# Split expert weights from DRAM tables, and a feed-forward that stays channel-major until its end

## The reference

```python
mod = (silu(c) @ wmod).reshape(32, 6, 1, 256)
sa, ca, ga, sb, cb, gb = ...          # ga, gb: magnitude at least 0.25
h = layernorm(x) * (1 + ca) + sa
S = scan(a * s + (1 - a) * h_t)       # along time
x = x + ga * (S @ W.T + b + depthwise_conv5(h) + conv_b)
h = layernorm(x) * (1 + cb) + sb
sel = argmax(softmax(gelu(h[:, -1] @ Wp1 + bp1) @ Wp2 + bp2))
g = gelu(h @ W1[sel] + b1[sel])       # 256 -> 512 channels
out = (g @ W2[sel] + b2[sel]) @ Wo + bo
x = x + gb * (h + 0.3 * out)
```

## Time and profile before

| | us |
|---|---|
| median of three runs (775.01 to 775.7) | 775.07 |
| span of the profiled execution | 773.5 |
| first up matmul of row 0 starts | 82.47 |
| first up matmul of row 31 starts | 754.22 |
| one row in the steady part (ACT's xn of 399.75 to that of 421.61) | 21.86 |

### The profile page before, as it was taken

The page is one execution under the profiler, slowest core; times in us unless marked ns, Lnnn a source line. Parts: engine busy times, 40 slices in busy tenths (PEclk is TensorE's granted clock), DMA queues, the critical chain, the costliest instruction groups (busy, mean ns, idle before and its releaser), DMA issues.

```text
span 773.5 us, 14701 instructions
## 1 busy us (share of the span) xinstructions
PE 703.6 (91%) x4343; PEld 589.4 (76%) x4343; DVE 656.7 (85%) x1357; ACT 540.6 (70%) x919; POOL 605.6 (78%) x556
## 2 busy tenths in 40 slices
PE   5987899999999999999999999999999999999986
PEld 5776777788777777888777777887777777887775
DVE  1777799999999999999999999999999999999821
ACT  1246877778777777787777777787777777787653
POOL 2003888888888988888898888888899888888775
PEclk9999999999999999999999999999999999999999
DMA  9630022211111121111111222101122221211011
GB/s 309 219 106 17 31 63 62 63 59 37 44 48 62 61 61 61 61 48 41 41 53 61 61 61 61 61 33 44 45 61 61 61 61 61 60 34 44 21 36 55
DMA packets 47391, 48.93 MB, mean 63 GB/s; under 512 B 2874, under 2 KB 44793, under 8 KB 47361
## 3 DMA queue, kind: packets, MB, share of 16 engines
q1 hardware_dynamic: 46736, 46.96, 19.6%
q10 hardware_dynamic: 624, 1.61, 0.6%
HBM read 31.73 MB, written 16.83 MB: 63 GB/s over the span
## 4 chain that ended last, share of the span: by engine, by line
POOL 35%; ACT 31%; issue 19%; PE 7%; ACTq 3%; DVE 3%; POOLq 1%; DMA 1%; DVEq 0%
ACT xn L442 15%; POOL up_w L393 9%; POOL down_w L403 9%; POOL rstd L367 7%; POOL ve L365 4%; ACT up_w L480 4%; ACT hid L542 3%; ACT hid_hi L548 3%; ACT g_hi L516 3%; ACT g L511 2%; POOL nmr L371 2%; ACTq L475 2%; PE Q L827 2%; POOL mr L369 2%; PE TR L797 1%
## 5 line engine op out<-in xcount | busy, mean ns | idle before, releaser
L642 DVE SCALAR_TENSOR_TENSOR Y<-h,taps,Y 128x512 f32<-128x512 f32 x320 | 226.4, 743 | 36.9 <-PE Y L933 33.3
L411 POOL TENSOR_TENSOR g_lo<-g,g_hi 128x512 fp32r<-128x512 f32 x128 | 161.2, 1279 | 1.6 <-ACT g_hi L516 1.6
L833 PE MATMUL Q<-down_w,g_lo 128*128 128x256 f32 x512 | 158.4, 309 | 0.0
L835 PE MATMUL Q<-down_w,g_hi 128*128 128x256 f32 x512 | 144.5, 282 | 0.0
L834 PE MATMUL Q<-down_w,g_hi 128*128 128x256 f32 x512 | 144.5, 282 | 0.0
L442 ACT ACTIVATE xn<-x,nmr,rstd 128x256 f32<-128x256 f32 x128 | 66.4, 589 | 87.9 <-POOL nmr L371 87.9
L393 POOL TENSOR_TENSOR up_w<-up_all,up_w 128x1024 fp32r<-128x1024 f32 x32 | 76.5, 2390 | 46.8 <-ACT up_w L480 46.8
L833 PE MATMUL U<-hid_hi,up_w 128*128 128x512 f32 x256 | 103.6, 405 | 0.0
L835 PE MATMUL U<-hid_hi,up_w 128*128 128x512 f32 x256 | 101.3, 396 | 0.0
L834 PE MATMUL U<-hid_lo,up_w 128*128 128x512 f32 x256 | 101.1, 395 | 0.0
L511 ACT ACTIVATE g<-U,b_w 128x512 f32<-128x512 f32 x128 | 87.4, 683 | 17.2 <-PE U L835 14.0
(11 more groups left out here) (115 smaller groups left out, 1584.2 us busy)
## 6 DMA issues: line engine op xcount, KB each, us to landing
x_sb<-in_L_attn_x_dram SPq DMA_DIRECT2D x32, 512.0 KB, 4.8
out_dram<-o_sb SPq DMA_DIRECT2D x64, 256.0 KB, 2.2
g<-in_L_ffn_W_dram SPq DMA_DIRECT2D x8, 512.0 KB, 4.3
up_all<-in_L_ffn_W_dram SPq DMA_DIRECT2D x1, 4096.0 KB, 16.8
gb_bc<-gate_table SPq DMA_DIRECT2D x32, 128.0 KB, 4.0
x<-in_L_wmod_dram ACTq DMA_DIRECT2D x2, 384.0 KB, 3.5
beta_w<-beta_table SPq DMA_DIRECT2D x32, 2.0 KB
xn<-in_L_wmod_dram ACTq DMA_DIRECT2D x1, 384.0 KB, 5.0
```

Source lines behind the costliest of these rows:

```text
L411: nc.gpsimd.tensor_tensor(g_lo[:, f], g[:, f], g_hi[:, f].bitcast(f32), ALU.subtract).then_inc(g_lo_ready, 1)
L642: ins = nc.vector.scalar_tensor_tensor(out=Y[c][:, :], in0=h[:, c, k:k + T], scalar=taps[:, c, k:k + 1], in1=Y[c][:, :], op0=ALU.mult, op1 ...
L833: mm(out_, w_lo, m_hi, start=start, stop=False)
L835: return mm(out_, w_hi, m_hi, start=False, stop=stop)
```

## The change

All per-row weight work moves to a set-up. For each expert ACT and POOL split W1 once, and the hi and lo parts are written by SP to a DRAM table `up_table` (1 MB per expert; its last columns hold b1 and 0.3 * (b2 @ Wo + bo)); the combined down weights are split by ACT and DVE and written to `down_table` (1 MB per expert). Per row, SP waits for the router and fetches both halves: two DMAs of about 1 MB into buffers that alternate by row.

The down product becomes channel by time: 24 matmuls of 512 columns, the start being four matmuls that add `hid_lo` and `hid_hi` through an fp32r identity. Gate and bias are applied by one ACT operation per half on the way out of PSUM (into `rT`), then eight PE transposes (t4) go back to times, and DVE adds x in place. x stays in one ring of six row buffers; `gate_table`, `modc`, `gb_bc`, `o_sb` and `x1` are gone.

The `lo` part of the scan moves from DVE to POOL. The norm's two trivial steps (add EPS, negate the mean) move from POOL to DVE, which leaves POOL two operations per norm. The loop is written out in full, slots -3 to 31, with the rows set one slot further ahead. The modulation is made by six fp32 matmuls of 512 columns and twelve transposes. The order inside the slot is new for every engine.

```diff
-EXPERTS_AT = {(-2, "middle"): (0,), (-1, "start"): (1, 2), (-1, "fill"): (3, 4), (-1, "middle"): (5,),
-              (0, "start"): (6,), (0, "fill"): (7,)}
+EXPERTS_AT = {(-3, "t1"): (0, 1), (-2, "t1"): (2, 3), (-2, "t2"): (4,),
+              (-1, "router"): (5,), (-1, "t1"): (6,), (-1, "t2"): (7,)}
...
+    for e in range(E):
+        split_out(e)
+        if e + 2 < E:
+            load_w1(e + 2)
...
+        if e in (1, 2, 3):
+            load_w2(e + 1)
+        if e == 5:
+            load_w2(5)
+    for e in range(4):
+        down_out(e)
+    load_w2(6)
+    sp.wait_ge(s_comb, 2 * 5)
+    load_x(3)
+    load_w2(7)
+    for e in range(4, E):
+        down_out(e)
...
+        wait(sp, up_done, FC * (r - 1))
+        wait(sp, gelu_out, FC * (r - 1))
+        wait(sp, gbeta_ready, r - 1)
+        wait(sp, down_done, DC * (r - 1))
+        sp.wait_ge(sel_ready, r + 1)
+        e = sp.value_load(sel8[0:1, par, 0:1], min_val=0, max_val=E - 1)
+        sp.dma_start(up_w[:, par].bitcast(f32), up_table[bass.ds(e, 1)].rearrange("o p n -> p (o n)")).then_inc(up_loaded[par], 16)
+        sp.dma_start(down_w[:, par].rearrange("p k n -> p (k n)").bitcast(f32),
+                     down_table[bass.ds(e, 1)].rearrange("o p n -> p (o n)")).then_inc(down_loaded[par], 16)
...
+        pool.wait_ge(stats_ready, r + 1)
+        wait(pool, used, TT * r)
+        nc.gpsimd.tensor_tensor(rstd[:, :], ve[:, :], minus_half[:, :], ALU.pow).then_inc(step, 1)
+        pool.wait_ge(step, r + 1)
+        nc.gpsimd.tensor_tensor(nmr[:, :], nm[:, :], rstd[:, :], ALU.mult).then_inc(ready, 1)
...
+    def slot(i):
+        if row(i + 3):
+            norm(i + 3, stats1_ready, xn1_ready, nm1, ve1, rstd1, nmr1, rstd1_step, norm1_ready)
+        if i == -3:
+            for e in range(4):
+                w1_lo(e)
+        if i == -2:
+            for e in range(4, E):
+                w1_lo(e)
+        if row(i):
+            g_low(i, 0)
+            g_low(i, 1)
+        if row(i + 1):
+            r = i + 1
+            wait(pool, up_done, FC * (r - 1))
+            for c in range(DC):
+                pool.wait_ge(hid_hi_ready, DC * r + c + 1)
+                nc.gpsimd.tensor_tensor(hid_lo[:, r % 2, c], hid[:, c], hid_hi[:, r % 2, c].bitcast(f32),
+                                        ALU.subtract).then_inc(hid_lo_ready, 1)
...
+            wait(pool, oT_ready, DC * i)
...
+            g_low(i, 2)
+            g_low(i, 3)
+        if row(i + 2):
+            norm(i + 2, stats2_ready, xn2_ready, nm2, ve2, rstd2, nmr2, rstd2_step, norm2_ready)
+        if row(i + 3):
+            r = i + 3
+            wait(pool, mix_done, DC * r)
+            for c in range(DC):
+                pool.wait_ge(S_hi_ready, DC * r + c + 1)
+                nc.gpsimd.tensor_tensor(S_lo[:, c], S[:, c], S_hi[:, c].bitcast(f32), ALU.subtract).then_inc(S_lo_ready, 1)
...
+        wait(act, s_comb, 2 * (e - 1))
+        if e == 6:
+            act.wait_ge(s_w1_lo, 7)
...
+    def slot(i):
+        if row(i):
+            g_high(i, 0)
+        if row(i + 1):
+            r = i + 1
+            wait(act, hid_lo_ready, DC * r)
+            for c in range(DC):
+                act.wait_ge(t3_done, DC * r + c + 1)
+                nc.scalar.activation(hid[:, c], TR[c][:, :], ACT.Identity, bias=col(SB + c, r),
+                                     scale=col(CB + c, r)).then_inc(hid_ready, 1)
+        if row(i):
+            gelu(i, 1)
+            g_high(i, 1)
+        if row(i + 1):
+            r = i + 1
+            act.wait_ge(r_nav, r + 1)
+            nc.scalar.activation(nav[:, :], TR[0][:, 0:1], ACT.Gelu, bias=vecs[:, V_BP1:V_BP1 + 1]).then_inc(nav_ready, 1)
+            wait(act, up_done, FC * (r - 1))
+            for c in range(DC):
+                act.wait_ge(hid_ready, DC * r + c + 1)
+                nc.scalar.copy(hid_hi[:, r % 2, c], hid[:, c]).then_inc(hid_hi_ready, 1)
+        for e in experts_at(i, "router"):
...
+        if row(i + 3):
+            r = i + 3
+            wait(act, t3_done, DC * (r - 1))
+            normalise(r, rstd1, nmr1, norm1_ready, xn1_ready)
+        if i == -3:
+            w1_hi(0)
...
+            w1_hi(1)
+            w2T_copy(0)
...
+        if row(i):
+            gelu(i, 2)
...
+            for c in range(DC):
+                act.wait_ge(t1_done, DC * r + c + 1)
+                wait(act, conv_done, DC * (r - 1) + c + 1)
+                nc.scalar.activation(h[:, c, PAD:PAD + T], TR[c][:, :], ACT.Identity, bias=col(SA + c, r),
+                                     scale=col(CA + c, r)).then_inc(h_ready, 1)
+        if i == -3:
+            w1_hi(2)
+        if i == -2:
+            w1_hi(4)
+            w1_hi(5)
+        for e in experts_at(i, "t1"):
+            expert(e)
+        if i == -3:
+            w1_hi(3)
+        if i == -2:
+            w1_hi(6)
+        if row(i + 2):
+            r = i + 2
...
+            wait(act, t4_done, HB * (r - 2))
+            for c in range(DC):
+                act.wait_ge(conv_done, DC * r + c + 1)
+                nc.scalar.activation(rT[:, c], Y[c][:, :], ACT.Identity, bias=col(GAB + c, r),
+                                     scale=col(GA + c, r)).then_inc(r1_ready, 1)
+        if i == -2:
+            w1_hi(7)
+        if row(i):
+            g_high(i, 2)
+            gelu(i, 3)
+            g_high(i, 3)
+        for e in experts_at(i, "t2"):
+            expert(e)
+        if row(i):
+            act.wait_ge(t2_done, HB * min(i + 3, B))
+            act.wait_ge(gbeta_ready, i + 1)
+            for c in range(DC):
+                act.wait_ge(down_done, DC * i + c + 1)
+                nc.scalar.activation(rT[:, c], Q[c][:, :], ACT.Identity, bias=gbeta[:, c:c + 1],
+                                     scale=col(GB + c, i)).then_inc(oT_ready, 1)
...
+            gelu(i + 1, 0)
+        if row(i + 2):
+            r = i + 2
+            wait(act, t1_done, DC * min(r + 2, B))
+            normalise(r, rstd2, nmr2, norm2_ready, xn2_ready)
...
+    def expert(e):
+        for k in range(2):
+            dve.wait_ge(s_down_hi, 2 * e + k + 1)
+            nc.vector.scalar_tensor_tensor(out=down_tab[:, e, 1, k * 512:(k + 1) * 512], in0=Q[k][:, :], scalar=OUT_SCALE,
+                                           in1=down_tab[:, e, 0, k * 512:(k + 1) * 512].bitcast(f32),
+                                           op0=ALU.mult, op1=ALU.subtract).then_inc(s_down_lo, 1)
...
+            dve.wait_ge(t2_done, HB * r + k + 1)
+            nc.vector.tensor_tensor(xr[:, r % NX, ts], xr[:, r % NX, ts], TR[k][:, :].rearrange("p (t d) -> p t d", d=D),
+                                    ALU.add).then_inc(x1_ready, 1)
+            dve.wait_ge(x1_ready, HB * r + k + 1)
...
+    def slot(i):
+        if row(i + 2):
...
+            conv(i + 2, 0, CONV_HEAD)
...
+            nc.vector.max_index(sel8[:, r % 2], top8[:, :], TR[0][0:1, 8:8 + E]).then_inc(sel_ready, 1)
+        if row(i + 2):
+            conv(i + 2, CONV_HEAD + CONV_MID, TAPS * DC)
+        for e in experts_at(i, "router"):
...
+        for e in experts_at(i, "t1")[:1]:
+            expert(e)
+        if row(i + 4):
+            stats1(i + 4)
+        for e in experts_at(i, "t1")[1:]:
+            expert(e)
+        if row(i + 2):
+            residual1(i + 2)
+        for e in experts_at(i, "t2"):
+            expert(e)
+        if row(i + 3) and i > -3:
+            scan(i + 3)
+        if row(i):
+            for k in range(HB):
+                ts = slice(k * TPB, (k + 1) * TPB)
+                dve.wait_ge(t4_done, HB * i + k + 1)
+                nc.vector.tensor_tensor(xr[:, i % NX, ts], xr[:, i % NX, ts], Q[k][:, :].rearrange("p (t d) -> p t d", d=D),
+                                        ALU.add).then_inc(o_ready, 1)
...
+    def down_hid(i):
...
+        wait(pe, o_ready, HB * i)
...
+        for c in range(DC):
+            mm(Q[c][:, :], ident_r[:, :], hid_lo[:, par, c], start=True, stop=False)
+            mm(Q[c][:, :], ident_r[:, :], hid_hi[:, par, c], start=False, stop=False)
...
+    def slot(i):
+        if row(i + 2):
+            mix(i + 2)
...
+        if row(i):
+            down_hid(i)
...
+        for e in experts_at(i, "router"):
+            expert(e)
+        if row(i):
+            down(i, 0)
+            up(i, 2)
+        if row(i + 3):
+            r = i + 3
+            wait(pe, sel_ready, r - 1)
+            to_channels(r, xn1_ready, t1_done)
+        for e in experts_at(i, "t1"):
+            expert(e)
+        if row(i):
+            down(i, 1)
+            up(i, 3)
+        if row(i + 2):
+            r = i + 2
+            pe.wait_ge(h_ready, DC * min(r + 2, B))
+            pe.wait_ge(r1_ready, DC * (r + 1))
+            to_tokens(TR, rT, t2_done)
+        for e in experts_at(i, "t2"):
+            expert(e)
+        if row(i):
+            down(i, 2)
+            down(i, 3)
+        if row(i + 1):
+            up(i + 1, 0)
+            up(i + 1, 1)
+        if row(i):
```

(33 more changed lines are left out.)

990 lines of the change are left out of this document (404 added, 586 removed).

## The result

The changed kernel takes 798.44 us in the median (796.78 to 799.16), the kernel before 775.35 beside it: a ratio of 1.0302 [1.0281, 1.0323], slower by 23 us. 788 had been forecast, with 754 to 812 as the range; sign, mechanism and range held, and the forecast was 10 us short.

The account below looks back on a forecast made before the run. No engine is full, so a chain across engines was taken to bound each row. First up 124 + 2, first interval 19.7, 29 rows 601.8, last interval 17.7, end 21.3: span 786.5, plus 1.6, 788 us; range 754 to 812.

Parts of the forecast that it names:

- sign: The whole kernel: slower than before by more than 0.2%, with a chance of 0.64.
- mechanism: Whole kernel: the rows give back 32 us, while set-up and ends take 45.
- PE's work in the set-up: Before the first up: each expert costs PE 3.5 us of matmuls and 0.87 of transposes.
- The cold PE behind the fetch: At the first ups: PE, idle before, starts at the lower clock, which adds 2 us.
- The row: Steady part: a chain across engines from one mix to the next takes 20.75 us per row against 21.86.
- the terms behind 11.0: From t2 to the next mix: t2's first half, statistics, DVE's two steps, POOL's norm, xn and t3's rest.
- the other side: From the start of mix to t2: 11.0 us through convolution, h and rT, nearly tied with PE's own 10.8.
- The norm runs undisturbed: Rival, POOL's norm beside DVE's scan: pow takes about 1 us, a row 19.6, total 755 us; chance 0.24.
- S_lo on POOL collides: Rival, between S_hi and mix: the lo part comes 1.3 us late, a row takes 22.0, total 825; chance 0.11.
- Slow table writes: Rival, set-up: table writes run at half rate, first up comes 17 us later, total 805 us; chance 0.12.
- The sides cancel: Rival, set-up against rows: loads never late, first up at 109, a row as forecast, total 773 us; chance 0.08.

Follow-up runs that it names:

- up_first: The changed kernel with row 0's up weights fetched ahead of the last two down-table writes; 785.5 us, 1.0151 of the kernel before.
- early_half: The changed kernel with the first half of the scan ahead of DVE's add, without a wait for POOL's norm; 768.27 us, 0.9916 of the kernel before.
- slo_dve: The changed kernel with both lo parts of the scan back on DVE, behind the hi parts; 789.49 us, 1.0198 of the kernel before.
- head_order: The changed kernel with W2(2) loaded ahead of the first table writes and S_lo(0) ahead of POOL's fourth w1_lo; 786.78 us, ratio 1.0161.
- best: The changed kernel with up_first, head_order, and the scan's first half ahead of DVE's add, the rest waiting for POOL's norm; 756.91 us, ratio 0.9768.

## Why the prediction was right, and where it was off

*The sign and the mechanism* were right: set-up against rows. Set-up was to cost 41.5 us up to the first up and costs 47.0.

*The term that was too small: PE's work in the set-up.* I priced an expert at 0.87 + 3.5 us, from rows at the higher clock, and put a term for the lower clock only behind the last wait. But PE waits again and again in the set-up. Experts 1, 5 and 6 on PE's timeline of the changed kernel, each with the transposes of the next W2 ahead of its matmuls, and the wait in mix(0):

```profile
37.72 1.97 PE L776 MATMUL U<-ident,xr 128*128 128x128 f32 x8 [10.09 <-DMA xr<-in_L_ffn_W_dram]
39.48 5.61 PE L825 MATMUL Q<-wo,g 128*128 128x256 f32 x16
44.74 0.58 PE L838 MATMUL Y<-S_hi,mix_w 128*128 128x512 f32 x1
...
50.35 0.80 PE L842 MATMUL Y<-S_lo,mix_w 128*128 128x512 f32 x1 [4.33 <-POOL S_lo L456]
...
96.79 1.97 PE L776 MATMUL U<-ident,xr 128*128 128x128 f32 x8 [1.57 <-DMA xr<-in_L_ffn_W_dram]
98.55 5.10 PE L825 MATMUL Q<-wo,g 128*128 128x256 f32 x16
...
106.89 1.04 PE L776 MATMUL U<-ident,xr 128*128 128x128 f32 x8
107.76 3.62 PE L825 MATMUL Q<-wo,w_raw 128*128 128x256 f32 x16
```

The windows of the same stretches (columns: window, length, busy time of each engine with its instructions, granted clock, DMA share, GB/s):

```profile
30.00:40.00 10.00, 2.28 (x10) 2.19 (x11) 3.22 (x12) 3.07 (x6) 2.34 (x1) 0.50 1.04 304
40.00:50.00 10.00, 6.02 (x20) 4.59 (x18) 1.38 (x2) 2.93 (x5) 3.26 (x2) 0.82 0.34 105
80.00:90.00 10.00, 6.74 (x28) 4.74 (x28) 5.51 (x8) 6.96 (x11) 3.76 (x5) 0.95 0.93 380
90.00:100.00 10.00, 7.68 (x30) 6.11 (x29) 7.17 (x13) 2.36 (x5) 4.49 (x5) 0.56 1.01 335
```

Expert 1 takes 7.0 us behind an idle PE. Its granted clock is 0.50, the level of 1.2 GHz, until 41.5, and 0.69 from there to its end. Expert 5 takes 6.8, again at 0.50 for its first 4 us. Expert 6, which starts at the higher level, takes the 4.4 that I had used. Followed against the forecast's own marks, the set-up goes like this:

| | forecast | measured | late by |
|---|---|---|---|
| W2(2) there (measured: in use) | 36 | 37.7 | 1.7 |
| expert 1 ends | 40 | 44.7 | 4.7 |
| S_lo(0) ends | 46.7 | 51.5 | 4.8 |
| conv(0) ends | 54 | 60.5 | 6.5 |
| W2(6) there (measured: in use) | 91.6 | 96.8 | 5.2 |
| expert 5 ends | 96 | 103.6 | 7.6 |
| expert 7 ends | 113 | 118.0 | 5.0 |
| first up | 124 | 129.4 | 5.4 |

The low clock accounts for 2.6 us at expert 1 (7.0 against 4.4, which the sum had as 4), some 1.7 at mix(0), whose last matmuls stand 0.43 apart instead of 0.23, and 2.4 at expert 5. A late load adds 1.7 at W2(2). Two terms went the other way. One was a misreading: I let W2(7) be issued only when expert 5 is done, but `load_w2` waits for the transposes of W2(5) alone, SP issues it at 87.20, and expert 6 does not wait for it, which gives back more than 2 us. What lies between conv(0) and W2(6) gives back 1.3. So part of the agreement is luck: errors of nearly 9 us are netted to 5.4. The late load may be chance too: up_first, the same kernel up to that point, has the transposes of W2(0) at 16.88 where the changed kernel has them at 18.59, and W2(2) in use at 35.70. Behind expert 7 the last table leaves, the fetch is issued at 124.52, and up begins 4.9 later, as forecast from two rows.

*The cold PE behind the fetch.* 2 us were priced. Row 0's first twelve matmuls stand 0.427 apart (129.44, 130.89, 132.17, in threes) and take 5.3 us to the next instruction at 134.73 instead of 2.8: 2.5. The Trainium skill (TensorE: Matmul & The Clock Gate, "What's actually happening") has the idle array begin at the lower clock; the trace agrees here and at experts 1 and 5 of the set-up (0.50 each), where I had not applied it. The first interval still came out 0.2 short of its 21.7, since the rest of it took 19.0 instead of 19.7.

*The row.* 20.75 was forecast and 20.90 measured. From t2 (419.73) to mix (429.46) 9.73 us stand against the 9.74 that the terms behind 11.0 add up to, so the whole of this side was right, with pow at 1.85. The product took 0.70 for 0.52; I had both beside the scan, but in the kernel before the product (414.95) stood beside DVE's lo parts (from 414.13), and here it stands behind the scan's second half. The rest is on the other side: from mix (408.54) to t2 (419.73) 11.19 instead of 11.0.

*The rivals.* "The norm runs undisturbed" did not come: the scan stood where it had stood. Its price was about right, though: early_half, where it does come, has a row 0.95 shorter. "S_lo on POOL collides" happens as described, 1.04 us on the second hi part, but in the slack: without it the row is the same (slo_dve). "Slow table writes" is refuted. "The sides cancel" needed loads in time; up_first (11.7 us) and head_order (10.9) show that reordering brings what it had priced at 15, and in best the first up comes at 104.83, ahead of its 109.

*What I had not seen* is why the rows gain at all. I had read the shorter row as the two norm steps less on POOL's chain; in the kernel before that same edit loses 64 us, since it lets g_lo into DVE's hi and lo parts. In the changed kernel g_lo stays away from them, and not because of the lo parts on POOL: in slo_dve, where these are back on DVE (417.75 to 419.03), g_lo begins at 420.18 all the same, behind the norm of another row and a wait of 1.09 us for ACT's g_hi. As far as the rows show, the new order of the slot keeps them apart. Which part of the change makes up the 0.95 us per row no run isolates.

## What to carry to other kernels

Before moving small steps between DVE and POOL, read which instruction each of them has running when the other issues one; a wait that puts them in order, or a short instruction put ahead of a long one, was worth 74 us and 30 us here (the 30 together with the early scan). A table that a later step must find complete is priced by the queue's order ahead of its last write, and matmuls between waits by a row at the lower clock. When one link of a chain is shortened, ask what was just as late beside it: the same move of S_lo was worth nothing per row, then 8 us.
